# Gated attention and expert block on one core: routing slots, GpSimd's order and the record sends rearranged

## The reference, cut to what matters

```
x    : 128 x 64 tokens of 128 numbers;  ctx the same shape
x    = x + tanh(g_xattn) * attention(layernorm(x), ctx, ctx)     # 16 heads of 8, 64 keys a sequence
h    = layernorm(x)                                              # 8192 tokens
gates = softmax(h @ w_red @ wg_n.T);  e = argmax(gates);  score = max(gates)
o    = gelu(h @ W1[e] + b1[e]) @ W2[e] + b2[e]                   # 8 experts, hidden 256, one expert a token
x    = x + tanh(g_ffn) * score * o
```

## Time and profile before

| | |
|---|---|
| median of the runs | 363.32 us |
| the profiled execution: its own time, its span | 366.57 us, 364.8 us |
| busy share PE, VectorE, ScalarE, GpSimd | 86%, 79%, 66%, 73% |
| chain that ended last, by engine | PE 44%, GpSimd 17%, VectorE 16%, issue 8%, ScalarE 8% |
| record sends | 64, 63.5 us in all, 993 ns each |
| scatters | 71, 70.0 us in all, 986 ns each |
| granted TensorE clock, mean | 0.935 |

### The profile page before, as it was taken

One profiled execution on the slowest core, in us unless ns is written; L12 is line 12 of the kernel. 1 busy time (PEld: TensorE's weight loads), 2 busy tenths in 40 slices (PEclk: granted clock), 3 DMA queues, 4 the chain that ended last, 5 costly groups with the idle time before them and its releaser, 6 DMA issues.

```text
span 364.8 us, 15361 instructions
## 1 busy us (share of the span) xinstructions
PE 314.0 (86%) x5630; PEld 237.8 (65%) x5630; DVE 286.6 (79%) x1031; ACT 240.4 (66%) x604; POOL 268.1 (73%) x349
## 2 busy tenths in 40 slices
PE   3879899999998999999998977865987999999950
PEld 1526657766775676676675655644966999999840
DVE  7675798889899999999898998877677666666630
ACT  3653889989898888998989964544433555555520
POOL 6482963684796898998899877587657777777771
PEclk9965999999999999999999996796799999999995
DMA  5344255334322423224212121162124433433210
GB/s 115 102 135 130 83 124 145 93 110 109 119 68 87 149 76 115 92 73 127 66 53 80 49 73 51 43 163 68 49 78 120 141 111 109 118 103 96 67 40 0
DMA packets 47157, 34.01 MB, mean 93 GB/s; under 512 B 9800, under 2 KB 42955, under 8 KB 47083
## 3 DMA queue, kind: packets, MB, share of 16 engines
q1 hardware_dynamic: 42440, 23.90, 23.1%
q0 software_dynamic: 4352, 9.00, 7.4%
q10 hardware_dynamic: 292, 0.13, 0.2%
HBM read 17.13 MB, written 10.04 MB: 74 GB/s over the span
## 4 chain that ended last, share of the span: by engine, by line
PE 44%; POOL 17%; DVE 16%; issue 8%; ACT 8%; SPq 2%; DMA 1%; POOLq 0%; DVEq 0%; ACTq 0%
PE m L1344 10%; PE sc L1254 9%; POOL records L403 6%; POOL xn L378 4%; PE sc L1132 4%; DVE mx L987 3%; PE m L1306 3%; PE pv L1207 3%; PE pv L1213 2%; ACT PT L601 2%; PE sc L1142 2%; PE sc L1125 2%; PE sc L1246 2%; PE m L1341 2%; ACT PT L599 2%
## 5 line engine op out<-in xcount | busy, mean ns | idle before, releaser
L987 DVE TENSOR_REDUCE mx<-sc 128x8 f32<-128x512 f32 x128 | 82.3, 684 | 18.0 <-PE sc L1142 17.7
L474 POOL DMA_INDIRECT out<-fo,rr x71 | 70.0, 986 | 23.1 <-issue 19.3
L403 POOL DMA_INDIRECT records<-XR,pos x64 | 63.5, 993 | 19.2 <-issue 16.2
L599 ACT ACTIVATE PT<-sc 128x512 f32<-128x512 f32 x64 | 38.1, 596 | 24.6 <-issue 19.2
L1344 PE MATMUL m<-w,fgT 128*128 x284 | 50.7, 302 | 0.1
L1254 PE MATMUL sc<-fxT,w1s 128*128 128x128 f32 x284 | 45.9, 286 | 4.5 <-DVE w1s L975 3.8
L1058 DVE SCALAR_TENSOR_TENSOR fo<-m,rr 128x128 f32<-128x128 f32 x71 | 24.9, 350 | 29.9 <-PE m L1344 29.9
L1207 PE MATMUL pv<-PT,V 128*32 128x64 f32 x2048 | 43.6, 227 | 5.4 <-DVE XR L999 4.8
L378 POOL TENSOR_SCALAR xn<-XC,mv,rstd 128x128 f32<-128x128 f32 x56 | 44.4, 802 | 0.0
L1254 PEld LDWEIGHTS sc<-fxT,w1s 128*128 128x128 f32 x284 | 39.0, 199 | 6.5 <-ACT fxT L581 4.2
L581 ACT ACTIVATE fxT<-sc 128x128 f32<-128x128 f32 x71 | 19.7, 277 | 34.8 <-PE sc L1246 34.8
(11 more groups left out here) (208 smaller groups left out, 700.7 us busy)
## 6 DMA issues: line engine op xcount, KB each, us to landing
rr<-records SPq DMA_DIRECT2D x71, 72.0 KB, 1.9
XC<-in_x SPq DMA_DIRECT2D x16, 256.0 KB, 4.0
C<-in_ctx SPq DMA_DIRECT2D x16, 256.0 KB, 3.9
Qd<-Qf SPq DMA_DIRECT2D x64, 64.0 KB, 1.9
Kd<-kb SPq DMA_DIRECT2D x64, 32.0 KB
w<-in_L_ffn_W SPq DMA_DIRECT2D x16, 128.0 KB, 2.7
out<-fo,rr POOLq DMA_INDIRECT x71, 2.3
w1l<-in_L_ffn_W SPq DMA_DIRECT2D x8, 128.0 KB, 3.9
```

The costliest lines, as they stand in the source:

```text
L403: nc.gpsimd.indirect_dma_start(out=records, out_offset=bass.IndirectOffsetOnAxis(ap=pos[:, u:u + 1], axis=0), in_=XR[:, u, :], in_offset=N ...
L474: nc.gpsimd.indirect_dma_start(out=out_rows, out_offset=bass.IndirectOffsetOnAxis(ap=rr[q][:, R_ID:R_ID + 1].bitcast(U32), axis=0), in_=fo ...
L599: nc.scalar.activation(pt[:, 0:2], sc[:, 0:2, 256:512], ACT.Exp)
L987: nc.vector.tensor_reduce(mx[c % 2][:, t:t + 2, HI * u:HI * u + HI], sc[:, t:t + 2, 0:256].rearrange("p t (i k) -> p t i k", i=HI), AX_X, ...
```

## The change

Three things move; no computation is added or removed.

1. Routing of groups 0 to 3 is packed from slots r+12, r+13, r+14, r+17, r+18 and r+19 (r+18 for group 3), with r the group's end, to r+11, r+12, r+12, r+13, r+14 and r+15. `whole_tiles`' five parts hang on group 3's count slot (61 before, 57 after) with new offsets: slots 61, 62, 66, 67, 68 become 57, 58, 61, 62, 66.
2. On GpSimd `gate_norm(s-4)` stands ahead of `norm(s+1)`.
3. The table of sends begins in step 7 and runs ahead: 2 tiles sent by the end of step 7, 6 by step 8 (before: 4), 30 by step 14 (28), 39 by step 15 (36), 47 by step 16 (44), 55 by step 17 (52), 60 by step 18 (60).

```
     if g <= LISTED:
-        return r + 12, r + 13, r + 14, r + 17, r + 18, r + (19 if g < LISTED else 18)
+        return r + 11, r + 12, r + 12, r + 13, r + 14, r + 15
...
-        sends = {8: (0, 4), 9: (3, 1), 10: (3, 1), 11: (3, 1), 12: (3, 1), 13: (3, 1), 14: (3, 1), 15: (8, 0), 16: (4, 4),
-                 17: (4, 4), 18: (1, 7)}
+        sends = {7: (0, 2), 8: (1, 3), 9: (1, 3), 10: (1, 3), 11: (1, 3), 12: (1, 3), 13: (1, 3), 14: (1, 3), 15: (2, 7), 16: (3, 5),
+                 17: (4, 4), 18: (1, 4)}
...
                     send(sent, sent + before)
+                if s >= 4:
+                    gate_norm(s - 4)
                 if 2 <= s + 1 < NC:
                     norm(s + 1)
                 if s == 2:
                     constants()
-                if s >= 4:
-                    gate_norm(s - 4)
...
-                for part, at in enumerate((listed, listed + 1, listed + 5, listed + 6, listed + 7)):
+                for part, at in enumerate((listed, listed + 1, listed + 4, listed + 5, listed + 9)):
```

## The result

The changed kernel takes 375.04 us (median of four runs, 373.31 to 377.03), the kernel before in the same comparison 363.94 us (363.27 to 365.42). The ratio is 1.0336, with a 95% interval of [1.028, 1.0392]: slower by 3.4%, outside the forecast's range. The direction of the forecast was right (+2.8), its size was not (+11). The profiled execution of the changed kernel took 377.03 us, 10.5 more than the one of the kernel before. The experiments ran on several chips: on that of e5 to e8 the kernel before took 361.77 us, on those of e1 to e4 and e9 to e18 it took 437 to 447 us, and every kernel traced there was slow from some 115 us on. Of these, only the ratio against the kernel before and the first 115 us are read, and later steps only against one another.

The account below looks back on a forecast made before the run. Both phases' ends were taken to hang on the chain through group 6's line 860, which waits for gate_norm(14). Terms -1.5 + 0.8 + 1.9 + 1.6 = +2.8 gave 366.1 us; own range 364.5 to 368.7, 361.2 to 368.8 leaving out 2 in 10.

Parts of the forecast that it names:

- a: Steps 7 to 14: gate_norm moves for free and step 9's spread starts on time; -1.5 us, between 0 and 2.0 gained.
- b: VectorE's moved routing and list work up to group 4's gate in slot 67; +0.8 us, bounds 0 and +1.6.
- c: GpSimd between the gates of groups 4 and 5: sends queued behind group 4's gate delay gate_norm(13); +1.9 us.
- d: Between group 5's gate and gate_norm(14): sends 52 to 55 now all stand there; +1.6 us.
- R1: From slot 64 on, an even pace keeps TensorE's clock at 2.4 GHz; not slower, 361.3 or 360.0 us; chance 0.22.
- R2: Slots 70 and 72: waits of c and d bring TensorE's clock down; +1.3 us per tile, 368.0; chance 0.12.
- R3: TensorE's count comes one slot behind pick and line 1179 waits for it; +2.0 us, 368.1; chance 0.08.
- R4: Sends beside VectorE stretch, 0.18 us for each of twelve from tile 44 on; +2.1 us, 368.2; chance 0.03.

Follow-up runs that it names:

- e5: The kernel before with gate_norm ahead of norm and nothing else; 367.33 us against 361.77, ratio 1.0161.
- e8: The kernel before with the change's packed routing slots and list offsets alone, sends and gate_norm as they were; 396.24 us against 361.77, ratio 1.0923.
- e1: The changed kernel with gate_norm put back behind norm; 458.45 us against 446.63 for the kernel before, ratio 1.0281.
- e4: The changed kernel with the running totals of sends from step 15 on as in the kernel before; 450.68 us against 446.63, ratio 1.0105.
- e9: The changed kernel with fold_bias in quarters, one ahead of each of norm's xn instructions; 448.04 us against 441.23 for the kernel before, ratio 1.0098.
- e18: e4's kernel with group 3's slots and the lists' offsets back to the old ones; 443.13 us against 437.41 for the kernel before, ratio 1.0112.
- e10: The changed kernel with fold_bias whole but given a single input; 446.35 us against 441.23 for the kernel before, ratio 1.0115.
- e16: e5's kernel with fold_bias in quarters spread over norm's xn instructions; 442.18 us against 439.86 for the kernel before, ratio 1.0095.
- e7: The changed kernel with the running totals of sends from step 15 on as in the kernel before; 372.26 us against 361.77, ratio 1.0265.
- e6: The changed kernel with each fold_bias as four quarter instructions back to back; 378.13 us, ratio 1.0404 to the kernel before.
- e3: The changed kernel with each fold_bias as four quarter instructions back to back; 454.69 us, ratio 1.0168 to the kernel before.

## Why the prediction was wrong

**The step that failed is one that a and b share**: work that is only moved is priced at the durations it had in the trace of before. In a it is the word "free" for `gate_norm`'s move, and "only reordered"; in b, VectorE's moved work, it is "cost the same instructions". a and b had -0.7 us together. Measured between the two profiles, from step 6 to the mS of step 17, it is 7.0: 3.5 in steps 6 and 7, 0.7 in steps 8 to 13 and 4.0 in step 14, less 1.2 in steps 15 and 16. By terms, a (steps 7 to 13) measured +2.6 where it had -1.5, b (steps 14 to 16) +2.8 where it had +0.8, and step 6's 1.6 stood in no term. The main part of the first 3.5 is shown: e5 has 2.3 of it with `gate_norm`'s place alone, and e9 and e10 take more than half of it away with the held time, e16 1.6 of e5's 2.3.

Of step 14's 4.0 us the trace gives the parts, and no run isolates them at the usual pace: 1.2 of held line 860, 2.0 of VectorE's instructions that came in from slots 61 and 62 (15.36 us busy in 53 instructions against 12.13 in 39, less the hold), and 0.8 more of idle time in the wake behind it, at a clock of 0.90. VectorE had 1.14 us to spare there; I had used that as cover, and it was none: the idle time grew. The other side of the exchange gave back 0.8 in step 15 (VectorE's 12.63 us busy became 11.82), because the third and fourth of the lists' five parts moved into slots 61 and 62 in their turn, and nothing in step 16 (13.14 and 13.18 us busy). So the moved instructions by themselves come to +1.2, inside b's bounds of 0 and 1.6. What the bounds left out is the hold and the wake; for step 14 that is read from one trace and argued, not shown by a run. e7 against e5 agrees with it in size: 3.2 us more in step 14. The windows that this rests on, before and then after, from the mS of step 16 on to that of step 17 and to line 860 of group 6 (columns as in the earlier trace rows):

```profile
216.77:231.59 14.82, 12.46 (x263) 9.24 (x267) 13.14 (x49) 6.74 (x20) 9.89 (x12) 0.67 0.14 44
231.59:246.66 15.07, 9.58 (x280) 7.23 (x277) 11.76 (x53) 8.11 (x24) 11.96 (x14) 0.99 0.41 114
```

```profile
224.61:239.03 14.42, 9.18 (x263) 6.80 (x267) 13.18 (x47) 6.74 (x20) 8.07 (x10) 0.96 0.20 59
239.03:258.44 19.41, 11.76 (x280) 9.35 (x278) 10.26 (x49) 8.10 (x24) 14.59 (x17) 0.76 0.33 94
```

**a** came in its mechanism and not in its gain. The spread of step 9 started 0.1 us behind the end of its mS instead of 2.0, and TensorE's waits for MD are gone from 124.6 to 203.2. But steps 8 to 13 took 13.24 us each in the changed kernel and 13.11 before, 0.7 more in all, beyond a's bound of 0 us gained. Two readings are open. One is that the late MD had not set their length, a's own lower bound; it was weighed by one step that took 12.89. The other is that the gain came and was eaten: VectorE was held there for 1.8 us more than before, about what a had promised, and steps 9 and 12, which got a packed place, took 13.67 and 13.61 us instead of 13.20 and 13.00. The other four steps (8, 10, 11 and 13) took 0.3 less together, holds included. No run takes these holds away at the usual pace.

**c and d** were right. Their own quantities came out as forecast: from group 4's gate to the end of gate_norm(13) it took 11.2 us (11.3 forecast; its own terms add up to 11.2), from there to the end of gate_norm(14) 9.2 (9.4 forecast). Forecast: a wait of 2 to 3 us at line 860 of group 5, more than 3 idle ahead of send 44, 1 to 2 ahead of send 52. Measured: 2.65, 4.93 and 1.73. The wait of group 6's line 860, 2.55, is below the "over 3" given. Their sum, 3.5, was measured as 3.3 between the two first profiles, from the mS of step 17 to the last group's gate, and 3.8 between the changed kernel and e7. The stretch from the last group's gate to the end of the last scatter is 89.05 us, against 89.3 forecast.

**The rivals.** R1 came for its first stretch and is as small as it was priced: step 16 has a clock of 0.96 instead of 0.67, and takes 14.42 us instead of 14.82 (priced 0.3 to 0.6). Its large part, the stretch ahead of the last group's gate, did not come. R2 came in its sign: in the stretch of c and d the clock is 0.76 instead of 0.99, so the low clock went from step 16 to there and, in part, to step 14. That stretch is 4.3 us longer (19.41 against 15.07), 0.8 above c and d, where R2 had 1.3 for each tile; the stretch behind it gives 1.1 back (258.44 to 278.47 against 246.66 to 267.76). R3 did not come: line 1179 waited for the pick 0.2 us, once. R4 had the right family and the wrong victim. Sends beside VectorE did not stretch, 995 ns mean against 993:

```profile
L403 POOL DMA_INDIRECT records<-XR,pos x64 | 63.7, 995 | 28.3 <-issue 15.5
```

The one who pays is VectorE, and the partner is GpSimd's arithmetic. The trace of before already had a row of a held VectorE: the gate's 667 ns beside the spread at 111.62, although line 874 has one tensor input and a column of scalars, not two tensors. I quoted it "the other way round", and did not ask which of GpSimd's long instructions would slide over which of VectorE's. The figure of 620 and 3100 ns that I took from the Trainium skill stands in the same page's section "A bandwidth-pool intuition that's wrong (but worth ruling out)", for a copy on VectorE, and does not bear on instructions like line 1009. The Trainium skill, "SBUF — State Buffer", section "Who interferes with whom", states this pair too: an instruction of VectorE with two SBUF inputs contends with one of GpSimd that reads SBUF, and whoever comes second is blocked for the other's whole instruction. e5's rows agree for two inputs on both sides, 2.31 us under 2.36. e6 goes beyond it (the hold lasts over four instructions), and e10 falls short of it (0.77 us under a one-input instruction of 2.79). So do the short instructions of GpSimd: its 128x4 power in `gate_norm` (line 389) has two inputs and runs for 1.04 us, and no line 1009 beside it took over 0.33 us.

## What to carry to other kernels

When an instruction of GpSimd is moved or put out of the way, everything behind it on GpSimd changes its phase against VectorE. List GpSimd's wide two-input instructions (here the residual, the spread and `fold_bias`) and VectorE's two-input ones, and see which of them will fall together: each meeting costs VectorE the rest of GpSimd's unbroken stretch of such instructions, and it shows as busy time, not as a wait. Look for it in an engine's total busy time at the same count of instructions. Look at more than one trace, as a few tenths of a us decide who meets whom. Where VectorE waits for another engine's product ahead of the instruction that feeds the pipeline, ask what the pipeline behind it pays: in e8 it was one and a half times the wait.

## What the runs showed of the hardware

- A VectorE instruction with two SBUF inputs is held by a wide two-input instruction of GpSimd. A 128x128 one of 0.29 us (line 1009) took 1.96 to 2.40 us under a 2.36 us subtraction (changed kernel, e5). A 128x96 one of 0.26 took 2.39 (e8, e1). In all twenty traces every line 1009 that fell inside such an instruction whole was held, to 0.15 us behind its end (or that of the last of quarters that ran back to back): 36 of 36 by the residual (0.64 to 1.30 us), 34 of 34 by `fold_bias` or its quarters (0.60 to 2.83), 12 of 12 by the spread (0.45 to 0.66).
- Two inputs alone do not do it: inside GpSimd's 128x4 power of 1.04 us (line 389) all 52 took 0.28 to 0.33 us. Inside an xn, which has one tensor input, 88 of 100 took 0.38 us or less and the longest 0.54.
- It is not only VectorE's two-input instructions: line 874, with one tensor input, took 0.67 us beside the spread in the kernel before and 0.57 in the changed kernel, against 0.24.
- The hold outlasts an instruction: line 1009 took 2.38 and 2.83 us through four quarters that ran back to back (e6), line 860 3.69 through the residual and `fold_bias` (e18) and 4.12 through the residual and four quarters (e3). With a one-input instruction between the quarters line 1009 took 0.61 to 0.84 (e9, e16).
- Under a one-input instruction of GpSimd, 2.79 us long, line 1009 took 0.77 us (e10, one meeting).
- GpSimd pays little when it is second: line 389 took 1.16 us instead of 1.04 at 94.11 in the kernel before, with line 1009 on VectorE from 94.08 to 94.37.
- An indirect DMA's issue on GpSimd was not stretched by VectorE's two-input instructions: 64 sends at 995 ns mean, 993 in the kernel before.
